# One-core kernel of attention, two mixtures of experts and a recurrence: tanh in PSUM, masked state spread by DMA, keys on ScalarE, new order on all engines

## What is computed

```python
x = x + attn_a(_layernorm(x), ...)   # gated linear attention + feed-forward (gelu)
x = x + ffn(_layernorm(x), router_w, expert_weights)
x = x + attn_b(_layernorm(x), A, B, C, W_out, b_out)
x = x + ffn(_layernorm(x), router_w, expert_weights)
# attn_a, per head (16 heads, 8 keys, 16 values), over time:
S = jnp.exp(gt)[..., None] * S + kt[..., None] * vt[..., None, :]
o = einsum('bhk,bhkv->bhv', qt, S)
# attn_b, over time, h of 16 values:
h = jnp.tanh(xb_t + h @ A.T)
y = hs @ C;  return y @ W_out.T + b_out
# ffn: 8 experts of 256x256, the best two of softmax(x @ router_w.T) weighted and summed
```

## Time and profile before

| | |
|---|---|
| Median of 3 runs | 2058.72 us (2046.99 to 2063.43) |
| The profiled execution, its own time | 2060.23 us |
| Its span, first to last instruction | 2058.3 us |
| Mean granted clock of TensorE in it | 0.921 of full |
| Busy: TensorE, VectorE, GpSimd, ScalarE | 87%, 77%, 55%, 46% |
| Instructions | 49764 |

### The profile page before, as it was taken

One profiled execution on the slowest core, in us unless ns is written; L12 is line 12 of the kernel. 1 busy time (PEld: TensorE's weight loads), 2 busy tenths in 40 slices (PEclk: granted clock), 3 DMA queues, 4 the chain that ended last, 5 costly groups with the idle time before them and its releaser, 6 DMA issues.

```text
span 2058.3 us, 49764 instructions
## 1 busy us (share of the span) xinstructions
PE 1788.0 (87%) x15176; PEld 1482.2 (72%) x15176; DVE 1587.9 (77%) x4909; ACT 956.7 (46%) x3532; POOL 1130.2 (55%) x1451
## 2 busy tenths in 40 slices
PE   4687899899888999989899898989989898988876
PEld 3576777777777777777777777777777777777654
DVE  4676788778888878888877887887888788876554
ACT  4344544445554444555445455544544554444321
POOL 4765566566556556565655665555565556554211
PEclk8787999999999999999999999999999999998888
DMA  4100000000000000000000000000000000000000
GB/s 128 35 27 16 12 27 27 26 25 15 20 15 25 25 25 24 15 20 17 25 25 25 23 18 18 18 25 25 25 25 13 18 20 26 21 22 6 6 6 11
DMA packets 73360, 47.89 MB, mean 23 GB/s; under 512 B 39088, under 2 KB 72528, under 8 KB 73168
## 3 DMA queue, kind: packets, MB, share of 16 engines
q1 hardware_dynamic: 71648, 45.35, 7.4%
q10 hardware_dynamic: 1648, 1.72, 0.3%
HBM read 30.28 MB, written 16.78 MB: 23 GB/s over the span
## 4 chain that ended last, share of the span: by engine, by line
PE 65%; DVE 20%; issue 8%; ACT 4%; DMA 1%; SPq 1%; DVEq 0%; POOL 0%; ACTq 0%; POOLq 0%
PE ps L1096 51%; DVE hs L750 8%; PE ps L1113 5%; DVE y L771 4%; PE ps L1141 3%; ACT h_whole L526 2%; PE ps L1397 1%; DVE oh L824 1%; PE ps L1150 1%; PE ps L1129 1%; PE ps L1131 1%; ACT h_lead L525 1%; DVE stage L781 1%; DVE st_f L760 1%; DVE yT L833 1%
## 5 line engine op out<-in xcount | busy, mean ns | idle before, releaser
L1096 PE MATMUL ps<-we,yT 128*128 128x512 f32 x3072 | 907.3, 441 | 1.3 <-DVE mv L766 1.3
L1096 PEld LDWEIGHTS ps<-we,yT 128*128 128x128 f32 x3072 | 597.0, 208 | 116.0 <-DVE mv L766 1.5
L750 DVE SCALAR_TENSOR_TENSOR hs<-h_whole,cst,h_lead 48x8 fp32r<-48x8 f32 x1024 | 364.3, 356 | 322.8 <-ACT h_whole L526 322.0
L525 ACT ACTIVATE h_lead<-ps 48x8 fp32r<-48x8 f32 x1024 | 173.7, 170 | 855.6 <-PE ps L1113 850.9
L1113 PEld LDWEIGHTS ps<-hs,aT 128*128 128x128 f32 x1024 | 207.1, 202 | 261.7 <-issue 236.5
L1113 PE MATMUL ps<-hs,aT 128*128 128x8 f32 x1024 | 224.0, 219 | 145.0 <-DVE hs L750 139.2
L396 POOL TENSOR_TENSOR part<-part 128x256 f32<-128x256 f32 x64 | 52.0, 812 | 448.0 <-ACT part L544 448.0
L781 DVE SCALAR_TENSOR_TENSOR acc<-ps,coef,acc 128x256 f32<-128x256 f32 x384 | 184.9, 482 | 11.9 <-POOL acc L398 1.8
L781 DVE SCALAR_TENSOR_TENSOR stage<-ps,coef,stage 128x256 f32<-128x256 f32 x384 | 183.4, 478 | 11.9 <-POOL stage L398 4.5
L435 POOL TENSOR_TENSOR orstd<-omean,mhalf 128x32 f32<-128x32 f32 x32 | 176.2, 5505 | 2.7
L467 POOL TENSOR_TENSOR sx<-osq,cst 32x512 f32<-32x512 f32 x128 | 168.9, 1319 | 7.6
(11 more groups left out here) (178 smaller groups left out, 3580.3 us busy)
## 6 DMA issues: line engine op xcount, KB each, us to landing
xin<-in_x SPq DMA_DIRECT2D x64, 128.0 KB
vrow<-vtok SPq DMA_DIRECT2D x32, 256.0 KB, 2.1
vx<-vrow SPq DMA_DIRECT2D x128, 64.0 KB, 2.0
xag<-in_x SPq DMA_DIRECT2D x64, 128.0 KB
out<-stage SPq DMA_DIRECT2D x64, 128.0 KB
stage<-in_experts SPq DMA_DIRECT2D x1, 2048.0 KB, 7.9
stage<-in_Wvg SPq DMA_DIRECT2D x1, 512.0 KB, 5.5
stage<-in_W SPq DMA_DIRECT2D x1, 512.0 KB, 4.5
```

Of the source, the lines that this page charges most:

```text
L525: a.activation(h_lead[:], ps[0:NB, BANK["RB"], k * B:(k + 1) * B], ACT.Tanh)
L750: v.scalar_tensor_tensor(hs[0:NB, :, k], h_whole[:], keeps_rest, h_lead[:].bitcast(F32), ALU.mult, ALU.subtract).then_inc(sem("rnn_h"), 1)
L1096: ins = t.matmul(dst, left(lp, c), right(rp, c), start=(n == 1), stop=(n == 3 * chunks))
```

## The change

- **Tanh in PSUM.** `h_whole` becomes 8 columns of PSUM bank RB, behind the 256 of the recurrence's input. ScalarE writes its second tanh there, and VectorE's state write reads one input from PSUM and one from SBUF.
- **State masked, spread by DMA.** `dstate` is multiplied by the head mask `blockmask` instead of the decay at the round's end. GpSimd keeps `elast` (the decay at the end of the round before) and makes `dec = emid*elast`, `smid = state*dec`, `state = smid + dstate`. `smid` has a tile of its own, and SP's `spread_state` copies it into `sx` with four DMAs, behind v's and ahead of the x loads.
- **Bias in the read-out.** Rows 64 and 96 of `hs` are ones and rows 64 and 96 of `cw` hold lead and rest of `bout`; `x2b` becomes a plain copy of `m1.acc`, on ScalarE.
- **Keys on ScalarE.** `kx` is four `activation`s with the mask as scale.
- **Affine in place.** `affine` writes back into its PSUM bank (no `hT`, `h2T`), and lead and rest read from there.
- **Order.** The bodies of all engines are written out in another order; scores, the state's update and the attention's output are cut into halves or quarters between steps. TensorE's loop starts at step 7 instead of 6, ScalarE's at state 11 instead of 28, VectorE's at state 23 instead of 29. `BANK_ORDER` changes by stage numbers, and by the readers `hTs`, `h2Ts` in place of `hT`, `h2T`.

```diff
-        hT, hTs = sb("hT", [P, KC, TOK]), sb("hTs", [P, 2, KC, TOK], F32R)
+        hTs = sb("hTs", [P, 2, KC, TOK], F32R)
...
-        smid = osq[:].rearrange("p h v -> p (h v)").rearrange("p (b c) -> p b c", b=B)
+        smid = sb("smid", [P, B, HQ * DV])
...
-        h_whole, h_lead = sb("h_whole", [NB, B]), sb("h_lead", [NB, B], F32R)
+        h_lead = sb("h_lead", [NB, B], F32R)
...
+        h_whole = ps[0:NB, BANK["RB"], TOK:TOK + B]
...
+            def spread_state():
+                for j in range(J):
+                    r = slice(32 * j, 32 * j + 32)
+                    sp.dma_start(sx[r, :, j * HQ * DV:(j + 1) * HQ * DV], smid[r]).then_inc(sem("sx"), 16)
...
+                    copied = value(sp, c2)
+                    sp.wait_ge(sem("pads_zero"), 1)
+                    sp.wait_ge(sem("O11"), past(c2 - 1))
+                    sp.wait_ge(sem("smid"), copied)
+                    spread_state()
...
-                    g.tensor_tensor(state[:], state[:], dec[:].unsqueeze(2).broadcast_to([P, B, HQ * DV]), ALU.mult).then_inc(sem("decayed"), 1)
...
-                    g.tensor_tensor(x2b[:], m1.acc[:], bout[:].unsqueeze(1).broadcast_to([P, TILES, D]), ALU.add).then_inc(sem("x2b"), 1)
...
+                    g.tensor_tensor(dec[:], emid[:], elast[:], ALU.mult).then_inc(sem("dec"), 1)
...
+                    g.tensor_tensor(state[:], smid[:], dstate[:], ALU.add).then_inc(sem("state"), 1)
...
+                    g.tensor_tensor(smid[:], state[:], dec[:].unsqueeze(2).broadcast_to([P, B, HQ * DV]), ALU.mult).then_inc(sem("smid"), 1)
...
-                    for j in range(J):
-                        r = slice(j * 32, j * 32 + 32)
-                        g.tensor_tensor(sx[r, :, j * HQ * DV:(j + 1) * HQ * DV], smid[r],
-                                             blockmask[r].unsqueeze(1).broadcast_to([32, B, HQ * DV]), ALU.mult).then_inc(sem("sx"), 1)
...
-                a.activation(h_whole[:], ps[0:NB, BANK["RB"], k * B:(k + 1) * B], ACT.Tanh).then_inc(sem("rnn_tanh"), 1)
+                a.activation(h_whole, ps[0:NB, BANK["RB"], k * B:(k + 1) * B], ACT.Tanh).then_inc(sem("rnn_tanh"), 1)
...
-                    ins = a.activation(dst[:, c, :], ps[:, bank, c * TOK:(c + 1) * TOK], ACT.Identity,
+                    ins = a.activation(ps[:, bank, c * TOK:(c + 1) * TOK], ps[:, bank, c * TOK:(c + 1) * TOK], ACT.Identity,
...
+                    for h in range(HQ):
+                        ins = a.activation(kx[:, :, h, :], bt(kt[:]), ACT.Identity, scale=headmask[:, h:h + 1])
...
+                    a.activation(x2b[:], m1.acc[:], ACT.Copy).then_inc(sem("x2b"), 1)
...
-                    v.tensor_tensor(kx[:], bt(kt[:]).unsqueeze(2).broadcast_to([P, B, HQ, TS]),
-                                         headmask.unsqueeze(1).unsqueeze(3).broadcast_to([P, B, HQ, TS]), ALU.mult).then_inc(sem("kx"), 1)
...
-                                         eq[:, :, TS - 1:TS].rearrange("p (i q) o -> p i q o", q=BQ).broadcast_to([P, TILES, BQ, HQ * DV]),
+                                         blockmask.unsqueeze(1).unsqueeze(1).broadcast_to([P, TILES, BQ, HQ * DV]),
```

More of the change, by code:

```diff
@@ new lines, in body @@
+                if live(it, 2):
+                    pool.wait_ge(sem("smid"), c2)
+                    pool.wait_ge(sem("dstate"), c2)
+                    g.tensor_tensor(state[:], smid[:], dstate[:], ALU.add).then_inc(sem("state"), 1)
+                if live(it, 3):
+                    pool.wait_ge(sem("res"), c3)
+                    g.tensor_tensor(res[:], res[:], xmid[:], ALU.add).then_inc(sem("res_mid"), 1)
+                if live(it, 1):
+                    pool.wait_ge(sem("dec"), c1)
+                    g.tensor_tensor(elast[:], eq[:, :, TS - 1], one[:, 0:1].broadcast_to([P, B]), ALU.mult).then_inc(sem("elast"), 1)
@@ L884, in body @@
                 if live(it, 5):
[L885 to L895 removed]
+                    split_state(2, c5)
                 if live(it, 1):
@@ L939, in body @@
                     split_state(8, c5)
+                if live(it, 1):
+                    dve.wait_ge(sem("hT0"), c1)
+                    rest(hTs, by_chunk("Y0"), "hTs")
+                if live(it, 7):
+                    dve.wait_ge(sem("moe2"), c7 * GROUPS)
+                    combine(m2, 7, BANK["G2_7"], c7)
+                if live(it, 3):
+                    dve.wait_ge(sem("rstd_f"), c3)
+                    normed(y1, xmid, mv_f[:, :, 0], rf[:, 1, :]).then_inc(sem("y1"), 1)
+                if live(it, 5):
                     split_state(9, c5)
-                    split_state(10, c5)
                 if live(it, 4):
@@ L1415, in body @@
-                if live(it, 4):
-                    step(0, c4)
-                if live(it, 2):
-                    if isinstance(it, int) and it == 2:
+                if live(it, 5):
+                    step(0, c5)
+                if live(it, 2):
+                    free = [(name, value(pe, count)) for name, count in readers(it, "SD")]
+                    pe.wait_ge(sem("pads_zero"), 1)
+                    for name, count in free:
+                        pe.wait_ge(sem(name), count)
+                    pe.wait_ge(sem("kx"), c2)
+                    scores(0)
@@ new lines, in body @@
+                if live(it, 4):
+                    for name, count in readers(it, "F2"):
+                        pe.wait_ge(sem(name), count)
+                    pe.wait_ge(sem("gTs"), c4)
+                    product(ps[:, BANK["F2"], 0 * D:1 * D], lambda p, f: gTs[:, p, f, 0 * P:1 * P],
+                                  lambda p, f: wcols(W_2, p, f, D, 0, D), FB)
+                if live(it, 5):
+                    step(1, c5)
+                if live(it, 2):
+                    scores(1)
@@ L1419, in body @@
+                if live(it, 3):
+                    if isinstance(it, int) and it == 3:
                         pe.wait_ge(sem("weights_rest"), REST["router"])
```

889 lines of the change are left out of this document (435 added, 454 removed).

## The result

| | before | changed |
|---|---|---|
| Median, same chip | 2059.81 us | 1827.2 us (4 runs, 1826.51 to 1830.78) |
| Ratio, 95% interval | | 0.8884 [0.8844, 0.8924] |
| Span of the profiled execution | 2058.3 us | 1825.2 us |
| A round, first state to first state | 60.21 us | 52.12 us |
| TensorE at the lower clock, per round | 6.68 us | 0.0 us |

The last three lines are taken from the traces: the first hidden state of each round, and the time that the granted clock stood at half between that of the fifth round and that of the 28th.

What follows compares the result with a forecast made beforehand. No engine is full; a 60.2 us round holds 12.8 us beyond TensorE's own work. 47.4 + 4.8 + 0.5 + 0.6 + 0.75 = 54.05 us, 6.15 less over 31 rounds: 1870 us, range 1805 to 1990.

Steps and rivals of the forecast that it cites:

- TensorE's own 47.4: TensorE's own work in a round, summed from its timeline: 47.4 us, the same in both kernels.
- the walk's 4.8: Step-by-step walk through the new order: places where the state chain or VectorE's work exceeds TensorE's, 4.8 us a round.
- The residual 0.5: The same walk over the old order gave 59.75 us against 60.2 measured; the 0.45 was added as 0.5.
- The collision 0.6: VectorE's split of gT queues behind GpSimd's state sum, delaying TensorE's next state: 0.6 us a round, range 0 to 0.9.
- The clock 0.75: TensorE's lower clock left in the changed kernel: half of one fall a round, 0.75 us, range 0 to 2.9.
- y 1.95: VectorE's feed-forward y meets an idle GpSimd, 0.72 us for two operations instead of 2.67: 1.95 us a round less.
- State write 3.5: VectorE's hidden-state write always takes 0.22 us instead of 0.356 in the mean: 3.5 us a round less on the path.
- The keys at 0 and the spread state at 0: ScalarE's key operations and the DMAs spreading the state are both hidden behind other work: 0 us a round.
- 1, two falls a round: Rival: TensorE's clock still falls twice a round, 2.9 us instead of 0.75, 1937 us; chance 0.17.
- 3, the spread state late: Rival: the spread state reaches TensorE's attention late; at 11 us lateness 2122 us, slower; chance 0.09.
- 4, the write no shorter: Rival: VectorE's state write gets no shorter, +3.5 us a round, 1979 us; chance 0.05.
- 2, ScalarE's hand-offs late: Rival: three ScalarE hand-offs each 1 us late a round, 1963 us, chance 0.13; twice that, 2055 us, chance 0.06.

Runs made afterwards that it cites:

- before_psum: The kernel before with one edit, ScalarE's whole tanh written to PSUM instead of SBUF: 1885.3 us, ratio 0.9168.
- before_busy: The kernel before with six useless 512-column matmuls on TensorE ahead of its wait for the feed-forward's y: 1994.9 us, ratio 0.9702.
- before_both: The kernel before with two edits, whole tanh in PSUM and GpSimd waiting for the feed-forward's y before going on: 1807.3 us, ratio 0.8802.
- before_ywait: The kernel before with one edit, GpSimd waiting for the feed-forward's y before res, state product and x2b: 1951.1 us, ratio 0.9499.
- after_sx_pool: The changed kernel with the state spread by GpSimd's four masked products again instead of the four DMAs: 1894.3 us, ratio 0.9215.

## Why the prediction was right, and where it was off

**The size of the miss.** Forecast 54.05 us a round, measured 52.12: 1.93 less, 60 us over 31 rounds. The rest goes against it: the filling took 5.2 us more than before (145.6 against 140.4), the draining 1.4 more, and the shorter rounds at the ends gained 11 us less than 31 full ones would have; 60 - 18 = 42.

**Term by term.**
- *TensorE's own 47.4 and the walk's 4.8*: together 52.2, measured 52.12. That the sum is right to 0.1 us is in good part luck, for its places are not. An interval that holds one MoE group is 1.50 us where nothing else holds it up (before steps 23, 26, 29). The walk wanted 0.5 more before step 10 and 0.85 more before step 20; measured are 1.59 and 1.68. It wanted 0.2 more before steps 22, 23 and 26 each; measured are 1.53, 1.50 and 1.50. A step that waits for its state begins 0.15 us after the state is written; so it is before steps 7, 8, 12, 13 and 20, as the walk had it, but steps 10, 17, 22, 23 and 26 begin 0.3 to 0.5 us after it. What makes up for this in the sum was not worked out. The rule of the walk, that VectorE's order sets some of the distances, holds: in the middle most of TensorE's idle time is for the state, 13.4 us in the 23 rounds.
- *The residual 0.5*, the difference of the walk to the kernel before, was carried over, and with 52.2 in the two terms ahead of it there was no room for it. As these hold errors that cancel, the runs do not show where it belonged.
- *The collision 0.6* did not take the form expected. The split of gT met the state sum, but it is GpSimd that paid most:

```profile
1024.97 1.64 DVE L856 TENSOR_TENSOR gTs<-gT,gTs 128x1024 fp32r<-128x1024 f32 x1
```

```profile
1024.26 1.27 POOL L462 TENSOR_TENSOR state<-smid,dstate 128x512 f32<-128x512 f32 x1
1025.49 2.27 POOL L465 TENSOR_TENSOR res<-res,xmid 128x512 f32<-128x512 f32 x1
```

  The split is 0.4 us longer than the 1.22 us that it takes in before_psum, where its mean is 1218 ns, and then `res`, issued behind it, takes 2.27 us for some 1.3. The step behind the split (31) begins at 1026.90 us, 0.15 after its state is written, and its interval is 1.72 us where a MoE group alone takes 1.50: at most 0.2 us a round. By the forecast's own rule the 0.9 would have come if the sum had just begun; it was more than half through.
- *The clock 0.75* was 0. Half of one fall a round was assumed to be left, for the lean stretch. before_busy shows that most falls behind y hung on the stall, and in the middle of the changed kernel, where TensorE idles for 0.34 us at most at a time, none is left. The short stalls alone do not explain it, as before_both idles for 0.43 us at most and still has falls; there the lump of scores and update stands ahead of them.
- *The clock's whole price*: 2.9 us forecast for the kernel before. At 0.44 us per microsecond of lower clock the 6.68 us cost 2.9.
- *y 1.95*: before_ywait gained 3.62 us, and 4.01 of lower clock went with it; 3.62 - 0.44 x 4.01 = 1.86.
- *State write 3.5*: before_psum gained 5.92 with 3.56 of lower clock, so 4.35 without the clock. Of that 0.74 is TensorE's shorter idle time ahead of y (1.70 to 0.96 us), which leaves 3.6; on top of before_ywait it is 4.67 with 1.93, so 3.8. The term was some 0.1 to 0.3 too small. Both edits: 8.29 with 5.94 gives 5.7 against the forecast 5.45.
- *The order itself saves nothing*, as forecast. By the forecast's own walks the excess is 4.0 before (59.75 less 47.4, 1.95, 3.5 and 2.9) and 4.8 after, so the order costs 0.8. before_both has the old order, a round of 51.92 and 0.74 us of lower clock, some 0.3 us of it; the changed kernel has 52.12 and none. So the new order and the moved work together cost 0.5 us a round, and 0.3 of that comes back by the clock.
- *The keys at 0 and the spread state at 0*: both hidden, as forecast. `smid` ends at 1031.93 us and TensorE's attention begins at 1041.30, 9.4 us later where the walk gave 6.7; no wait of the middle names `sx`. What the forecast did not see is that the moved work, had it stayed, would have cost 0.6 and 2.5 in the new order. It took the removed products as load on GpSimd, which has room, and gave no price to what they do to VectorE beside them.
- *The rivals.* 1, two falls a round: none in the middle. 3, the spread state late: no wait. 4, the write no shorter: 220 ns. 2, ScalarE's hand-offs late: VectorE does wait 1.1 us a round for `oTs` with state 0 behind it, but step 1 begins 0.8 us after that state, on other work. The tanh starts over 0.3 us after its matmul at steps 6, 18, 19 and 26 (0.67, 0.47, 0.79, 0.36), of which the forecast named only 26; of the steps behind them only 7 and 20 wait for the state, and their intervals are 1.53 and 1.68 us. By its words this sign of being wrong was met, though the 3 us that it stood for did not come.

**What missed by most** are the three allowances on top of the walk: residual 0.5, collision 0.6 and clock 0.75, together 1.85 us a round, of which at most 0.2 is found. They are nearly the whole 1.93, or 57 us. Of the other way, filling and draining moved by 5.2 and 1.4 us, within the 10 us that were allowed; that the rounds at the ends gain less, 11 us, was taken to be made good by a shorter chain there and was not.

Against before_both the changed kernel takes 12.8 us more to fill, which no run of its own separates. In that stretch TensorE's longest single wait is 15.0 us for `og`, where before_both has 12.2 us for it in three waits, and its waits for y are 13.5 us against 9.0. Whether the order or the moved work brings that stays open.

**On the pages.** The state write reads one operand from PSUM and takes 220 ns, and 221 with both in SBUF where no work of GpSimd stands beside it (the 358 writes of the kernel before). The surcharge for a PSUM source that the Trainium skill gives (VectorE: DVE Perf Modes, on the TRN2 errata), from which 1935 us was estimated, does not show. Nor does a cheaper write by ScalarE into PSUM (159 against 158 ns), which the Trainium skill has under ScalarE: Activation LUTs. What the trace does bear out is the Trainium skill's rule for the ports that VectorE and GpSimd share (SBUF — State Buffer, the section "Who interferes with whom"): an operation of VectorE with two SBUF inputs, or one such as `tensor_scalar` (y) in a mode that takes both ports, and one of GpSimd that reads SBUF shut each other out, and whichever is issued first keeps the other waiting to its end. That y runs in such a mode no trace shows. The write that ends with GpSimd's state sum and goes from 356 to 220 ns in the mean without its SBUF operand, 2.27 for 1.3 us in `res`, and the y of after_sx_pool that ends with the products are in line with that rule.

## What to carry to other kernels

Where a small link of a serial chain shows a mean well above its usual duration, look at what the other engines do in its slow instances, and take the link's operand out of the shared memory or keep the neighbour waiting, before any work is moved or reordered: five lines did here what a new order of all engines did. Price work on GpSimd at what it does to VectorE beside it, not at its own load. Count a stall of TensorE twice, once as it stands and once for the matmuls behind it at the lower clock, here 0.44 us per microsecond of it. And compare a forecast with the trace place by place: a sum that is right to 0.1 us can hide places that are wrong by 0.7.
